# Mixture-of-experts slots on one core: the transposes of the next slot's x moved from behind gate and up to the start of the slot, and the copy of x on ScalarE moved ahead of Silu

## The chip, the cores and the metric

The kernel runs on one core of a Trainium2 chip. The metric is the device time of one execution in microseconds (us). The numbers are the median of three executions and one profiled execution, whose trace is what the rows below are read from.

## The reference

Two layers on x of 8 x 256 tokens, 512 wide: grouped-query cross attention with a residual, and then a mixture of experts with a residual. The change is in the second. Cut to what matters:

```python
h = layernorm(x).reshape(2048, 512)
logits = h @ gate_w.T                        # 32 experts
w, sel = top 4 of the softmax, normalised
for e in range(32):
    g, u = h @ Wg[e], h @ Wu[e]              # 512 -> 192
    large += (silu(g) * u * cw_large[:, e]) @ Wd[e]
for c in range(16):                          # one per pair of experts
    small += (silu(h @ cWg[c]) * (h @ cWu[c]) * cw_small[:, c]) @ cWd[c]
out = x + large + 0.05 * small
```

Only the four chosen experts of a token have a weight that is not zero.

## The kernel before, in words

The kernel has three stages in one program: attention (`attention`), routing (`route`) and the experts (`experts`, lines 1226 to 1445), where the change lies. All tiles there are float32.

Routing sorts the 2048 x 4 pairs of token and expert into slots of 128 rows that all belong to one expert, and makes tables of them: `tok` and `dst` (which row of the normalised x a place of the slot reads, and which row of the output it adds to), `slot_e` (the slot's expert) and `slot_buf` (which of the NW = 4 weight buffers of `W` holds it). In this run there are 78 slots for 32 experts. The normalised x lies in memory as `xd`, with the 32 routing weights of the row behind its 512 columns.

A slot s goes through these steps; p is s modulo 2 and picks one of two buffers:

- GpSimd, `gather` (L1285): copies the slot's column of `tok` to an index tile (L1290) and issues an indirect DMA of 128 rows into `xg[p]` (L1293). From slot 2 on it first waits for `xt_full` and `wt_ready` of slot s - 2, since `xg[p]` is used by that slot until then.
- TensorE, `transpose_x` (L1393): waits until the gather has landed (`x_loaded[p]`), then four transposes of 128 x 128 into `xt_ps[p]` (L1396).
- ScalarE, `x_evac` (L1326): copies them to `xT[p]` (L1328).
- TensorE, `gate_up` (L1399): four products for gate into `g_ps[p]` and four for up into `u_ps[p]`, each 320 columns wide, 192 of the large expert and 128 of the small one (L1403). The expert's weights are 2 MB in `W`; `experts_ready` says that they are there.
- ScalarE, `silu` (L1330): Silu of gate into `sg[p]` (L1332), released by the last product of up.
- VectorE, `gated` (L1371): `weights_of` copies the slot's routing weights out of `xg[p]` to `wt[p]` (L1369), then a = up x sg (L1374, L1375).
- TensorE, `transpose_a` (L1409): three transposes of a into `at_ps` (L1412). VectorE, `at_evac` (L1359), copies them to `aT[p]` (L1361).
- TensorE, `down` (L1415): three products of 512 columns into `y_ps` (L1420), which then counts `slots_done`.
- ScalarE, `y_evac` (L1334): scales y by `wt[p]` into `yb[p]` (L1339) and counts `y_empty`.
- GpSimd, `add` (L1296): copies the slot's column of `dst` (L1299), waits for `y_empty` and until the scatter of the slot before has landed (`y_added`), and issues an indirect DMA that adds `yb[p]` to the output (L1307).

Each engine works through its own queue in the order written, and the engines meet at semaphores only. TensorE's order within its slot s (`slot`, L1425) is the transposes of a of slot s - 1, gate and up of slot s, the transposes of x of slot s + 1, down of slot s - 1. Between them it reads `slot_e` and `slot_buf` from the tables (L1426, L1427, L1434). ScalarE's (L1341) is Silu of slot s, the copy of x of slot s + 1, the copy of y of slot s - 1. VectorE takes the transposes of a of slot s - 1, then wt and a of slot s. GpSimd issues four gathers ahead in all and then, in turn, `add` of slot k and `gather` of slot k + 4. So in TensorE's slot k + 1 down of slot k ends, its scatter and then the gather of slot k + 4 follow, and x of slot k + 4 is transposed in TensorE's slot k + 3.

SyncE (L1262) loads an expert's weights as soon as `slots_done` has reached the last slot of the expert that used the buffer before: the same end of down that releases the copy of y.

The loops run over two slots a turn, the first two slots and the last steps are written out.

Of the kernel before, what the change touches and what calls it, by code (L numbers as in the profile page):

```python
# [1225 lines left out]
def experts(nc, ident, xd, out, tabs, wts, W, w_loaded):  # L1226
# [4 lines left out]
    with ExitStack() as ctx:  # L1231
# [29 lines left out]
        @block.sync  # L1261
        def _(sp):  # L1262
            def arrived(i, p):
                sp.wait_ge(w_loaded[p], i * DMA + DMA)
                sp.sem_inc(experts_ready, 1)

            for p in range(NW - 1):
                arrived(0, p)
            with sp.Fori(1, E_ // NW) as i:
                for p in range(NW):  # L1270

                    last = sp.value_load(cum_i[0:1, bass.ds(i * NW + p - NW, 1)], min_val=1, max_val=NS)
                    sp.wait_ge(slots_done, last)
                    load_expert(sp, wts, W, w_loaded, i, p)
                    arrived(i if p else i - 1, (p - 1) % NW)
            arrived(E_ // NW - 1, NW - 1)

        def count(eng):

            return (eng.value_load(turns[0:1, 0:1], min_val=E_ // 2, max_val=NS // 2),  # L1280
                    eng.value_load(turns[0:1, 1:2], min_val=E_ - 2, max_val=NS - 2))
# [42 lines left out]
        @block.scalar  # L1324
        def _(act):
            def x_evac(s, p):  # L1326
                act.wait_ge(xt_full, s + 1)
                act.copy(xT[p][:, :, :], xt_ps[p][:, :].rearrange("p (c t) -> p c t", c=C)).then_inc(xt_empty, 1)  # L1328

            def silu(s, p):  # L1330
                act.wait_ge(gu_full, s + 1)
                act.activation(sg[p][:, :], g_ps[p][:, 0:IW], ACT.Silu).then_inc(sg_ready, 1)  # L1332

            def y_evac(s, p):  # L1334
                act.wait_ge(slots_done, s + 1)
                act.wait_ge(wt_ready, s + 1)
                if not (isinstance(s, int) and s < 2):
                    act.wait_ge(y_added, (s - 1) * DMA)  # L1338
                act.activation(yb[p][:, :], y_ps[:, :], ACT.Copy, scale=wt[p][:, :]).then_inc(y_empty, 1)  # L1339

            def slot(s, p, first=False):  # L1341
                silu(s, p)
                x_evac(s + 1, 1 - p)
                if not first:
                    y_evac(s - 1, 1 - p)

            x_evac(0, 0)
            slot(0, 0, first=True)
            slot(1, 1)
            n, last = count(act)  # L1350
            with act.Fori(1, NS // 2) as i:
                with act.If(i < n):
                    slot(i * 2, 0)
                    slot(i * 2 + 1, 1)
            y_evac(last + 1, 1)
# [35 lines left out]
        @block.tensor  # L1391
        def _(pe):
            def transpose_x(s, p):  # L1393
                pe.wait_ge(x_loaded[p], (s - p) * (DMA // 2) + DMA)
                for c in range(C):
                    m = pe.transpose(xt_ps[p][:, c * P:(c + 1) * P], xg[p][:, c * P:(c + 1) * P], ident[:, :])  # L1396
                m.then_inc(xt_full, 1)

            def gate_up(s, p, buf):  # L1399
                pe.wait_ge(xt_empty, s + 1)  # L1400
                for ps_, g in ((g_ps, 0), (u_ps, 1)):
                    for c in range(C):
                        m = pe.matmul(ps_[p][:, 0:IW], xT[p][:, c, :],  # L1403
                                      W[:, bass.ds(buf, 1), (2 * c + g) * IW:(2 * c + g + 1) * IW]
                                      .rearrange("p a f -> p (a f)"),
                                      start=(c == 0), stop=(c == C - 1))
                m.then_inc(gu_full, 1)

            def transpose_a(s, p):  # L1409
                pe.wait_ge(a_ready, s + 1)  # L1410
                for c in range(3):
                    m = pe.transpose(at_ps[:, c, :], a[p][:, c * P:(c + 1) * P], ident[:, :])  # L1412
                m.then_inc(at_full, 1)

            def down(s, p, buf):  # L1415
                pe.wait_ge(at_empty, s + 1)
                if not (isinstance(s, int) and s == 0):
                    pe.wait_ge(y_empty, s)
                for c in range(3):
                    m = pe.matmul(y_ps[:, :], aT[p][:, c, :],  # L1420
                                  W[:, bass.ds(buf, 1), GW + c * D:GW + (c + 1) * D].rearrange("p a d -> p (a d)"),
                                  start=(c == 0), stop=(c == 2))
                m.then_inc(slots_done, 1)

            def slot(s, p, first=False):  # L1425
                e = pe.value_load(slot_e[0:1, bass.ds(s, 1)], min_val=0, max_val=E_ - 1)  # L1426
                buf = pe.value_load(slot_buf[0:1, bass.ds(s, 1)], min_val=0, max_val=NW - 1)  # L1427
                if not first:
                    transpose_a(s - 1, 1 - p)
                pe.wait_ge(experts_ready, e + 1)  # L1430
                gate_up(s, p, buf)
                transpose_x(s + 1, 1 - p)
                if not first:
                    down(s - 1, 1 - p, pe.value_load(slot_buf[0:1, bass.ds(s - 1, 1)], min_val=0, max_val=NW - 1))  # L1434

            transpose_x(0, 0)
            slot(0, 0, first=True)
            slot(1, 1)
            n, last = count(pe)
            with pe.Fori(1, NS // 2) as i:  # L1440
                with pe.If(i < n):
                    slot(i * 2, 0)
                    slot(i * 2 + 1, 1)
            transpose_a(last + 1, 1)
            down(last + 1, 1, pe.value_load(slot_buf[0:1, bass.ds(last + 1, 1)], min_val=0, max_val=NW - 1))
# [58 lines left out]
```

## Time and profile before

| what | value |
|---|---|
| three executions | 1132.22 us median (1127.34 to 1135.8) |
| profiled execution | 1135.69 us |
| its span, first to last instruction | 1133.9 us |
| mean granted clock of TensorE in the span | 0.961 |
| TensorE busy (matmuls) | 1032.1 us (91%) |
| VectorE, ScalarE, GpSimd busy | 418.6, 349.3, 297.2 us |
| the expert stage | from about 510 us to the end |

How to read it: the span is cut into 40 slices of 28.3 us, and a digit is the busy share of an engine in that slice in tenths. PE is TensorE's matmuls, PEld its weight loads, DVE VectorE, ACT ScalarE, POOL GpSimd, SPq the queue of SyncE, which issues DMAs. A row of a timeline gives the start and the length of a piece in us from the span's start, the engine, the line, the operation, the tile written and those read, the number of instructions, and in brackets how long the engine was idle ahead of it and what ended that. The chain of waits goes back from a last instruction, at each step to what released it; "issue" in it is time in which an engine waited for nothing that the profile shows. A transpose on TensorE is a matmul with `ident`. In a row on stretches stand, behind the stretch and its length, the busy time of PE, PEld, DVE, ACT and POOL, the granted share of TensorE's full clock, the share of the DMA engines and GB/s. "to landing" is from the issue of a DMA to its semaphore.

### The profile page before, as it was taken

To read this page: it belongs to the slowest core of one execution; us is meant where nothing else is said; L and a number is where in the kernel's file an instruction comes from. 1 tells how busy PE (TensorE), PEld (TensorE's weight loads), DVE (VectorE), ACT (ScalarE), POOL (GpSimd) and SP (SyncE) were. 2 spreads that over 40 slices of the span, in tenths; PEclk is the share of its full clock that TensorE was granted. 3 is DMA by queue.
4 is the path that set the end of the run, shared out by engine and by line. 5 is a ranking of instruction groups with operands and counts; after the bars stand their busy time and mean duration, and the time that the engine had idled before them with its cause. 6 is when DMAs were issued, how large, how long until landed. Compare 5 with 4: busy or idle time off the path is not lost.

```text
span 1133.9 us, 19012 instructions
## 1 busy us (share of the span) xinstructions
PE 1032.1 (91%) x5518; PEld 664.7 (59%) x5520; DVE 418.6 (37%) x1039; ACT 349.3 (31%) x643; POOL 297.2 (26%) x387
## 2 busy tenths in 40 slices
PE   7689999999998979427999999999999999999995
PEld 6556666666665437215666666666665666666662
DVE  4476667766666524691111111111111111111110
ACT  2245454454545533141222222222222222222221
POOL 2101101011020000202344334334333344433432
PEclk9799999999999998757999999999999999999998
DMA  6433032130320003922765675675666667667443
GB/s 206 151 90 71 21 90 57 34 71 21 90 57 16 2 1 134 378 103 47 218 151 141 215 224 143 212 224 146 189 171 148 207 162 209 189 171 219 73 67 56
DMA packets 51449, 146.65 MB, mean 129 GB/s; under 512 B 9552, under 2 KB 18896, under 8 KB 47056
## 3 DMA queue, kind: packets, MB, share of 16 engines
q1 hardware_dynamic: 32192, 99.43, 26.3%
q0 software_dynamic: 17632, 42.74, 19.4%
q10 hardware_dynamic: 1584, 3.93, 1.0%
q8 instruction: 26, 0.43, 0.2%
q14 instruction: 15, 0.12, 0.0%
HBM read 100.73 MB, written 29.36 MB: 115 GB/s over the span
## 4 chain that ended last, share of the span: by engine, by line
PE 53%; issue 0%; DMA 0%; POOL 0%; ACT 0%; DVE 0%; POOLq 0%; ACTq 0%
PE y_ps L1420 18%; PE g_ps L1403 15%; PE u_ps L1403 15%; PE xt_ps L1396 3%; PE at_ps L1412 2%; DMA xg<-xd,gidx 0%; POOL out_x L1307 0%; ACT yb L1339 0%; ACT xT L1328 0%; DVE aT L1361 0%; ACT sg L1332 0%; DVE a L1374 0%; DVE a L1375 0%; POOL gidx L1290 0%; ACTq L1338 0%
## 5 line engine op out<-in xcount | busy, mean ns | idle before, releaser
L1420 PE MATMUL y_ps<-W,aT 128*128 x468 | 215.6, 597 | 1.1 <-DVE aT L1361 0.8
L1307 POOL DMA_INDIRECT out_x<-yb,yidx x78 | 125.3, 1606 | 297.2 <-DMA out_x<-yb,yidx 134.9
L348 ACT ACTIVATE pt<-stp 128x512 f32<-128x512 f32 x256 | 139.2, 597 | 169.4 <-PE stp L638 169.4
L470 DVE TENSOR_REDUCE mx<-s 128x2 f32<-128x512 f32 x256 | 163.0, 681 | 63.7 <-PE s L624 63.5
L1403 PE MATMUL g_ps<-W,xT 128*128 x624 | 183.3, 437 | 0.9 <-ACT xT L1328 0.9
L1403 PE MATMUL u_ps<-W,xT 128*128 x624 | 181.3, 434 | 0.0
L1403 PEld LDWEIGHTS u_ps<-W,xT 128*128 128x128 f32 x624 | 119.1, 191 | 49.9 <-issue 0.8
L1403 PEld LDWEIGHTS g_ps<-W,xT 128*128 128x128 f32 x624 | 113.5, 192 | 39.0 <-issue 2.4
L1374 DVE TENSOR_TENSOR a<-u_ps,sg 128x192 f32<-128x192 f32 x78 | 27.9, 358 | 291.5 <-ACT sg L1332 291.5
L1420 PEld LDWEIGHTS y_ps<-W,aT 128*128 128x128 f32 x468 | 83.5, 192 | 77.4 <-issue 77.3
L1332 ACT ACTIVATE sg<-g_ps 128x320 f32<-128x320 f32 x78 | 34.1, 437 | 306.2 <-PE u_ps L1403 306.2
L1361 DVE COPY aT<-at_ps 128x384 f32<-128x384 f32 x78 | 43.5, 558 | 183.3 <-PE at_ps L1412 183.3
L1339 ACT ACTIVATE yb<-y_ps,wt 128x512 f32<-128x512 f32 x78 | 53.7, 688 | 167.7 <-PE y_ps L1420 167.7
L624 PE MATMUL s<-kst,qst 96*128 96x256 bf16 x512 | 85.9, 277 | 20.4 <-DVE mx L470 19.6
L1293 POOL DMA_INDIRECT xg<-xd,gidx x80 | 80.9, 1011 | 69.8 <-POOL gidx L1290 65.8
L638 PE MATMUL stp<-qst,kst 98*128 98x256 bf16 x512 | 78.5, 276 | 8.5 <-DMA qst<-nm 8.2
L624 PEld LDWEIGHTS s<-kst,qst 96*128 96x128 bf16 x512 | 44.3, 98 | 61.8 <-DVE mx L470 41.2
L638 PEld LDWEIGHTS stp<-qst,kst 98*128 98x128 bf16 x512 | 45.2, 98 | 42.3 <-issue 33.6
L1290 POOL COPY gidx<-tok 128x1 uint32 (+1 forms) x80 | 58.4, 731 | 40.3 <-POOLq L895 29.6
L654 PE MATMUL ov<-pt,vx 128*32 128x256 f32 x1024 | 68.5, 385 | 0.0
L682 PE MATMUL side<-Wfc,oT 128*128 128x512 f32 x128 | 61.9, 599 | 1.5 <-ACT oT L338 1.5
L261 POOL TENSOR_TENSOR q<-qres,q 128x512 bf16<-128x512 f32 x14 | 16.2, 1158 | 161.7 <-DVE q L464 161.7
(172 smaller groups left out, 949.5 us busy)
## 6 DMA issues: line engine op xcount, KB each, us to landing
W<-in_wts SPq DMA_DIRECT2D x32, 2048.0 KB, 8.2
qst<-q SPq DMA_DIRECT2D x42, 256.0 KB, 4.9
ctxT<-in_ctx SPq DMA_DIRECT2D x8, 512.0 KB, 3.5
xd<-r_xn SPq DMA_DIRECT2D x16, 256.0 KB, 2.0
out_x<-xs SPq DMA_DIRECT2D x1, 4096.0 KB, 13.9
kst<-k SPq DMA_DIRECT2D x48, 64.0 KB, 2.1
xs<-in_x ACTq DMA_DIRECT2D x1, 2560.0 KB, 11.2
qst<-nm SPq DMA_DIRECT2D x128, 2.0 KB
```

Source lines behind the costliest of these rows:

```text
L348: act.activation(pt[g % 2][:, 2 * (j % 2) + r, :, :], stp[n % STP][:, :, :], ACT.Exp, scale=DH ** -0.5).then_inc(exp_done, 1)
L470: dve.tensor_reduce(mx[j // CH % 2][:, h:2 * G:G], s1[r][:, :, :], AX.X, ALU.max)\
L624: m = pe.matmul(s1[r][:, t, :], qst[b % 2][0:ROWS_QK, head(j, r), t * P:(t + 1) * P], kst[b % 2][0:ROWS_QK, head(j, r) // C, :], start=Tru ...
L638: m = pe.matmul(stp[n % STP][:, t, :], kst[b % 2][0:ROWS_ST, head(j, r) // C, t * P:(t + 1) * P], qst[b % 2][0:ROWS_ST, head(j, r), :], st ...
L654: m = pe.matmul(ov[c * VW:(c + 1) * VW, g % 2, :], vx[b % 2][:, t, g % 2 * C + c, :], pt[(b * G + g) % 2][:, c, t, :], start=(t == 0), sto ...
L682: m = pe.matmul(side[:, :], oT[t][:, c, :], Wfc[:, c, :], start=(c == 0), stop=(c == C - 1))
L1290: pool.tensor_copy(idx[p][:, :], tok[:, bass.ds(s, 1)]).then_inc(idx_ready, 1)
L1293: pool.indirect_dma_start(xg[p][:, :], None, xd[:, :], bass.IndirectOffsetOnAxis(idx[p][:, :], 0))\
L1307: pool.indirect_dma_start(out[:, :], bass.IndirectOffsetOnAxis(yidx[p][:, :], 0), yb[p][:, :], None, compute_op=ALU.add).then_inc(y_added, ...
L1339: act.activation(yb[p][:, :], y_ps[:, :], ACT.Copy, scale=wt[p][:, :]).then_inc(y_empty, 1)
L1403: m = pe.matmul(ps_[p][:, 0:IW], xT[p][:, c, :], W[:, bass.ds(buf, 1), (2 * c + g) * IW:(2 * c + g + 1) * IW] .rearrange("p a f -> p (a f) ...
L1420: m = pe.matmul(y_ps[:, :], aT[p][:, c, :], W[:, bass.ds(buf, 1), GW + c * D:GW + (c + 1) * D].rearrange("p a d -> p (a d)"), start=(c == ...
```

## The change

Two lines change places with others. On TensorE the transposes of x of slot s + 1 go from between `gate_up` and `down` to the start of the slot, ahead of the transposes of a. On ScalarE the copy of x of slot s + 1 goes ahead of Silu of slot s. Gathers, scatters, weight loads and all waits inside the steps are as they were.

```diff
@@ scalar @@
             def slot(s, p, first=False):
+                x_evac(s + 1, 1 - p)
                 silu(s, p)
-                x_evac(s + 1, 1 - p)
                 if not first:
                     y_evac(s - 1, 1 - p)
@@ tensor @@
                 buf = pe.value_load(slot_buf[0:1, bass.ds(s, 1)], min_val=0, max_val=NW - 1)
+                transpose_x(s + 1, 1 - p)
                 if not first:
                     transpose_a(s - 1, 1 - p)
                 pe.wait_ge(experts_ready, e + 1)
                 gate_up(s, p, buf)
-                transpose_x(s + 1, 1 - p)
                 if not first:
                     down(s - 1, 1 - p, pe.value_load(slot_buf[0:1, bass.ds(s - 1, 1)], min_val=0, max_val=NW - 1))
```

On TensorE, in the first of the two slots of the loop's body, this stands before the change from the last product of up on: the transposes of x (`xt_ps`), the read of the weight buffer's number, the products of down (`y_ps`), the reads for the next slot and its transposes of a (`at_ps`).

```order
L1403 MATMUL u_ps<-W,xT 128x320
L1394 ISA
L1396 MATMUL xt_ps<-ident,xg 128x128 x4
L1434 ISA
L1434 TENSOR_LOAD slot_buf
L1434 ISA x2
L1420 ISA
L1420 MATMUL y_ps<-W,aT 128x512
L1420 ISA
L1420 MATMUL y_ps<-W,aT 128x512
```

At the start of the same slot after the change, from the read of the weight buffer's number to the first product of gate (`g_ps`):

```order
L1427 TENSOR_LOAD slot_buf
L1427 ISA x2
L1394 ISA
L1396 MATMUL xt_ps<-ident,xg 128x128 x4
L1412 MATMUL at_ps<-ident,a 128x128 x3
L1431 REGISTER_ALU
L1400 REGISTER_ALU
L1403 ISA
L1403 MATMUL g_ps<-W,xT 128x320
```

The four transposes of x have moved to the front of the slot, in front of the three of a; the ones of a and all products behind them now follow the wait for the gather, which stands in front of L1396.

On ScalarE, in the same slot, before the change Silu (`sg`) is first:

```order
L1331 ISA
L1332 ACTIVATE sg<-g_ps 128x320
L1327 REGISTER_ALU
L1328 COPY xT<-xt_ps 128x512
L1338 ISA
L1339 ACTIVATE yb<-y_ps,wt 128x512
```

and after it the copy of x (`xT`) is first:

```order
L1327 ISA
L1328 COPY xT<-xt_ps 128x512
L1331 REGISTER_ALU
L1332 ACTIVATE sg<-g_ps 128x320
L1338 ISA
L1339 ACTIVATE yb<-y_ps,wt 128x512
```

The copy of y stays last.

## Rows read from the trace of the kernel before

**Rows 1.** the page: busy tenths in 40 slices; a DMA issue, us to landing
```profile
PE   7689999999998979427999999999999999999995
...
W<-in_wts SPq DMA_DIRECT2D x32, 2048.0 KB, 8.2
```

**Rows 2.** the chain of waits, 799 to 835 us: start us, us, what
```profile
801.45 0.33 PE at_ps L1412 x3
...
806.09 0.44 PE xt_ps L1396 x4
...
809.10 0.33 PE at_ps L1412 x3
```

**Rows 3.** timeline: start us, us, engine line op out<-in xcount [idle before <-releaser]
```profile
809.22 0.69 ACT L1339 ACTIVATE yb<-y_ps,wt 128x512 f32<-128x512 f32 x1 [2.07 <-PE y_ps L1420]
...
855.13 0.69 ACT L1339 ACTIVATE yb<-y_ps,wt 128x512 f32<-128x512 f32 x1 [2.07 <-PE y_ps L1420]
...
855.19 0.34 SPq L886 DMA_DIRECT2D W<-in_wts  x1
...
856.40 0.15 DVE L1369 COPY wt<-xg 128x1 f32 x1 [0.47 <-issue]
856.82 1.61 POOL L1307 DMA_INDIRECT out_x<-yb,yidx  x1 [3.31 <-ACT yb L1339]
...
859.48 1.01 POOL L1293 DMA_INDIRECT xg<-xd,gidx  x1 [0.85 <-POOL gidx L1290]
...
867.22 0.42 PEld L1396 LDWEIGHTS xt_ps<-ident,xg 128*128 128x128 f32 x4 [0.43 <-DMA xg<-xd,gidx]
...
867.40 1.60 POOL L1307 DMA_INDIRECT out_x<-yb,yidx  x1 [6.71 <-DMA out_x<-yb,yidx]
```

**Rows 4.** timeline where the expert stage begins
```profile
511.08 1.17 POOL L1293 DMA_INDIRECT xg<-xd,gidx  x1 [1.00 <-POOL gidx L1290]
...
514.85 1.12 PE L1396 MATMUL xt_ps<-ident,xg 128*128 128x128 f32 x4 [6.73 <-DMA xg<-xd,gidx]
...
516.00 0.59 ACT L1328 COPY xT<-xt_ps 128x512 f32<-128x512 f32 x1 [8.44 <-PE xt_ps L1396]
...
516.84 1.43 PE L1403 MATMUL g_ps<-W,xT 128*128 x2 [0.87 <-ACT xT L1328]
```

**Rows 5.** 520 to 1120 us: who waited for whom; landing of yb's scatters
```profile
PEld xt_ps L1396 <- DMA xg<-xd,gidx: 0.4, 1, 0.4
...
DMA to landing us min/median/max: 4.7/5.0/9.7
```

**Rows 6.** timeline of GpSimd, 815 to 875 us
```profile
841.52 1.61 POOL L1307 DMA_INDIRECT out_x<-yb,yidx  x1 [3.79 <-ACT yb L1339]
...
844.18 1.01 POOL L1293 DMA_INDIRECT xg<-xd,gidx  x1 [0.85 <-POOL gidx L1290]
...
849.66 1.60 POOL L1307 DMA_INDIRECT out_x<-yb,yidx  x1 [4.28 <-DMA out_x<-yb,yidx]
```

**Rows 7.** the chain of waits, 860 to 885 us: start us, us, what
```profile
862.66 0.33 PE at_ps L1412 x3
...
867.29 0.58 PE xt_ps L1396 x4
867.88 0.25 issue
...
871.09 0.54 PE at_ps L1412 x3
...
878.99 0.33 PE at_ps L1412 x3
```

**Rows 8.** tile W: duration ns min/median/max, first to last start
```profile
L886 SPq DMA_DIRECT2D W<-in_wts x28: 337/341/365, 541.1 to 1040.5; - x28
```

**Rows 9.** two stretches: busy us and instructions of each engine, PEclk, DMA
```profile
424.00:428.00 4.00, 0.10 (x1) 0.13 (x2) 3.03 (x22) 1.59 (x2) 2.11 (x12) 0.88 0.06 18
428.00:434.00 6.00, 6.00 (x27) 4.56 (x28) 1.94 (x5) 1.76 (x3) 0.35 (x1) 0.51 0.51 194
```

## The prediction

> **What bounds the kernel now.** I read the page's slices first. From slice 20 of 40 (about 540 us, early in the expert stage) TensorE stands at nine tenths or more in every slice but the last [rows 1]: this stage has no idle time to win back. The chain of waits over one slot [rows 2] shows why: it is TensorE alone, without a gap, three transposes of a (0.33 us), gate and up (from 801.78 to 806.09, 4.31), four transposes of x (0.44), down (from 806.53 to 809.10, 2.57), 7.65 us from one at_ps to the next. There are 78 slots. So the change can only win if something else becomes shorter, and its danger is a wait put in front of TensorE, which works in its written order.
>
> Which wait ends last once x is wanted at the slot's start? I followed one x row set back on the timeline [rows 3]. A slot boundary (the end of down) lies 0.12 us ahead of yb's copy, from 809.10 in [rows 2] against the copy at 809.22; here 855.13 - 0.12 = 855.01. Call it T. GpSimd has one queue: scatter of slot k, then the index copy and the gather for slot k + 4. The scatter waits for yb(k), which down(k) releases at T, the end of slot k + 1. It issues at 856.82 (T + 1.8), the gather at 859.48 (T + 4.5). Its x is transposed in slot k + 3. Before, that is behind gate and up of slot k + 3, at T + 7.65 + 0.33 + 4.31 = T + 12.3; after, at the start of that slot, T + 7.65. The slack for a landing falls from 12.3 - 4.5 = 7.8 us to 3.2 us.
>
> What a landing takes: the first gather, with no other kernel work on the engines, is issued at 511.08 and TensorE starts on it at 514.85, 3.8 us later [rows 4]. The gather of [rows 3], issued 4.3 us behind a 2 MB weight load (855.19), needs 867.22 - 859.48 = 7.7 us. Even the shortest is beyond 3.2. Before, the second just fits: in the whole stage TensorE waited for a gather once, 0.4 us [rows 5].
>
> **The change part by part.** It removes and adds no matmul or copy. The slot's 7.65 us of work are the same; so is the work on ScalarE.
>
> Copy of x ahead of Silu: price 0. The transposes that release it now end 4.3 us ahead of up, so Silu is still released by up, and the copy takes its place in ScalarE's idle time. Queued behind it are Silu and the copy of y; the y copy waits for down at the slot's end anyway. It can't win either: the transposes of a are covered as before, by down and the x transposes.
>
> Transposes of x ahead of those of a: behind the new wait stand the transposes of a, gate and up and down, all of the slot. The gathers themselves do not come earlier. Their buffer is free earlier, but what holds them is the scatter in front of them on GpSimd's queue, which hangs on the end of down.
>
> Slot without a weight load: landing at T + 4.5 + 3.8 = T + 8.3, wanted at T + 7.65, late by 0.6.
>
> Slot with a load: the load is released by the same end of down (855.19 beside the yb copy), lasts 8.2 us [rows 1], and so lies over scatter and gather. A usual one, also behind a load, is [rows 6]: the scatter of 841.52 holds the next one until 849.66. In [rows 3] the scatter of 856.82 holds its follower until 867.40, and the gather had landed at 867.22, 0.2 earlier. So a usual loaded gather lands about 849.66 - 0.2 = 849.5, which is 5.3 us after its issue at 844.18 (an estimate from those rows). T + 4.5 + 5.3 = T + 9.8, late by 2.1. Ends: 3.8 (no effect of the load) and 7.7. Scatters, from issue to landing, have a median of 5.0 and a maximum of 9.7 [rows 5], the latter being the one of [rows 3]; I take 5.3 for the usual ones. Six GpSimd waits for a scatter's landing are 5.6 us or longer (one of them stands in [rows 3], 6.71) where a usual one is 4.3 [rows 6]; for these six I add 1.7 us, late by 3.8.
>
> Restart: a TensorE queue that has run empty needs time to run ahead again. In [rows 7] the x transposes start on time (867.29) but their landing was just in time, and the two slots take 878.99 - 862.66 = 16.33 us instead of 15.30, 1.0 us lost: x transposes 0.58 instead of 0.44, 0.25 before down, where the weight buffer's number is read from a table, a transposes 0.54 instead of 0.33. In the new order 4.3 us of gate and up lie between the wait and that table read, so of these I take only 0.14 and 0.21 and a rest of 0.05: 0.4 per late landing; bounds 0 and 1.0.
>
> How lateness adds up: a gather hangs on the end of slot k + 1 and is wanted at the start of slot k + 3, so a wait at the start of slot k + 2 shifts the demand and not the gather. The wait of a slot is its lateness less the wait of the slot before. So a loaded slot pays fully (2.1 + 0.4 = 2.5), and the unloaded one behind it pays almost nothing. Almost, since GpSimd's index copy waits also for wt, which VectorE makes after the transposes of a (856.40 + 0.15, T + 1.5, after the change 0.44 plus the wait later); I put 0.15 on each slot behind a load. Unloaded slots in a row pay half of 1.0. There are 28 loads between 541 and 1041 us [rows 8], one in 2.3 slots: mostly every second, some every third. A third slot's wait is taken off the next loaded slot, so its sum is nothing.
>
> Start: transposes of x(1) now stand ahead of the first gate and up, at half clock, 1.1 us where the copy of x(0) leaves 0.8 free between 516.0 and 516.84 [rows 4]; the second gather was issued at about 513.3. I put 0.8; 0 to 2 bound it.
>
> Sum: 22 usual loads x 2.5 = 55; 6 long ones x (3.8 + 0.4) = 25; 28 slots behind loads x 0.15 = 4; about 12 unloaded slots at the ends x 0.5 = 6; start 1; what the kernel before loses in [rows 7] and two smaller places, -1 to -2. Together 90. The profiled execution took 1135.7 us, so 1225.7; it is 3.5 above the median of 1132.2, so about 1222 for a median.
>
> **The rivals.** First, the waits are smaller. With a restart of 0 and loaded landings of 4.5 us, between the two measured ones but near the short end, a loaded slot pays 4.5 + 4.5 - 7.65 = 1.3: 28 x 1.3 = 37 and nothing elsewhere, 1169. For it: GpSimd's times in a profile are rough. Against: 8.3 us for the unloaded landing come from two plain rows.
>
> Second, not slower: the landing of a lone gather is shorter than it looks in [rows 4], since the time from issue to start there holds TensorE's own waking too. The place is the start of every slot, the price 0 as long as a landing takes less than 7.65 - 4.5 - 0.4 = 2.8 us; then only the start is left, less the 1.0 us of [rows 7], 1132. Against: 3.8 and 7.7.
>
> Third, TensorE's clock falls. In [rows 9] TensorE does almost nothing for 4 us (424 to 428) and the next 6 us run at 0.51, the level of 1.2 GHz. Such a stretch costs 3 us. My six long waits are near 4 us: 6 x 3 = 18, 1240. If every load's wait did it, 28 x 3 = 84, 1306. Against: usual waits of 2.1 us stand between more than 7 us of work. The Trainium skill, TensorE: Matmul & The Clock Gate, section on HAM oscillation, holds that a wait for a DMA on every tile can throttle the array again so that each tile starts cold. By that rule the 28 or all slots would run partly at the low level; the trace before has no such repeated wait to test it.
>
> **How the numbers follow.** Forecast 0.72; smaller waits 0.11; clock 0.10; not slower 0.07. Within the forecast, restart 0 and the six long ones priced as usual ones take off 0.4 x 28 + 10 = 21 and lead to 1201; a restart of 1.0 adds 17, and half of the usual loads at the long price 19 more, 1258. To reach the rivals in part, the range is 1180 to 1260. A measurement here tells about 1% from no change. Faster by over 1% 0.02, within 1% 0.05, slower 0.93.
>
> **What would show it.** In the trace after: weight loads of TensorE for xt_ps end waits on the gather in most slots (some 50 of 78, about 60 to 80 us in all, against 0.4); slots with a load last about 10.2 us, those behind them 7.7 to 7.9; GpSimd's waits for the scatter's landing become rarer, since slots grow; gather issues stay 4.5 us behind the end of down; TensorE's digits fall from 9 to 8 in the loop. Wrong it would be if the xt_ps waits were few, if they occurred but the slots without loads stayed at 7.65 throughout, or if the granted clock left 1.0 between 530 and 1110 us.

## The result, and the profile after

The changed kernel takes 1214.78 us in the median of four executions (1213.48 to 1221.76), against 1131.64 before: a ratio of 1.0748, 95% interval 1.0703 to 1.0792, so 7.5% slower. The profiled execution took 1216.07 us, 80.4 more than the one before. The text on record says 1222, with a range of 1180 to 1260.

The page of the changed kernel, the two rows that answer to [rows 1] and the span:

```profile
span 1214.3 us, 19012 instructions
...
PE   7699999999999792398988889898989988998995
...
PEclk9899999999999986599999999999999999999998
```

From slice 20 on digits of 8 stand among the nines, where before there were nines only. Matmuls whose ends are modelled hide a part of the gaps, so the list of who waited for whom says more (us in total, times, longest; 520 to 1200 us, to be read beside [rows 5]):

```profile
PEld xt_ps L1396 <- DMA xg<-xd,gidx: 105.7, 54, 3.2
POOL out_x L1307 <- DMA out_x<-yb,yidx: 100.3, 23, 4.6
...
PE xt_ps L1396 <- DMA xg<-xd,gidx: 65.8, 44, 2.4
...
POOL gidx L1290 <- DVE wt L1369: 25.7, 28, 9.2
```

TensorE's matmuls stood idle for 65.8 us ahead of transposes of x, in 44 waits, and its weight loads for 105.7 us; before the change the latter were 0.4. The longest wait of a matmul was 2.4 us. The two lists count the same waits on two queues and are not to be added: what moves the time is the one of the matmuls. The scatters, for which GpSimd waited 134.9 us before, now cost it 100.3: slots are longer, and more of them have landed when the next is due. The index copy waits for wt in 28 cases; apart from a first one of 9.2 us before the loop, some 0.6 each.

How one slot looks, on the timeline from 803 to 822 us (start, length, what, and the idle time in front with its end):

```profile
803.84 0.60 PE L1396 MATMUL xt_ps<-ident,xg 128*128 128x128 f32 x4
...
808.46 1.01 POOL L1293 DMA_INDIRECT xg<-xd,gidx  x1 [0.84 <-POOL gidx L1290]
...
811.77 0.69 ACT L1339 ACTIVATE yb<-y_ps,wt 128x512 f32<-128x512 f32 x1 [2.22 <-PE y_ps L1420]
811.83 18.18 SPq L886 DMA_DIRECT2D W<-in_wts  x2
...
812.11 0.66 PE L1396 MATMUL xt_ps<-ident,xg 128*128 128x128 f32 x4 [0.46 <-DMA xg<-xd,gidx]
...
813.46 1.61 POOL L1307 DMA_INDIRECT out_x<-yb,yidx  x1 [3.79 <-ACT yb L1339]
...
816.12 1.01 POOL L1293 DMA_INDIRECT xg<-xd,gidx  x1 [0.85 <-POOL gidx L1290]
...
820.10 0.69 ACT L1339 ACTIVATE yb<-y_ps,wt 128x512 f32<-128x512 f32 x1 [2.22 <-PE y_ps L1420]
...
821.60 0.66 PE L1396 MATMUL xt_ps<-ident,xg 128*128 128x128 f32 x4 [1.62 <-DMA xg<-xd,gidx]
```

An unloaded slot first. The gather issued at 808.46 is wanted at the boundary, 811.77 - 0.12 = 811.65, and TensorE starts on it at 812.11, 3.65 us after the issue and 0.46 idle. Then a loaded one: the weight load starts at 811.83, the scatter at 813.46 (T + 1.8), the gather at 816.12 (T + 4.5, T = 811.65), and TensorE starts at 821.60, 5.5 us after the issue. The boundary is at 820.10 - 0.12 = 819.98; 1.62 us are lost. These two are usual ones: over the whole stage, of the gathers that TensorE waited for, the 28 behind a load account for 55.6 us of waits and the 16 others for 10.1. From issue to TensorE's start, 26 of the 28 take 5.3 to 5.6 us, and the 16 others have a median of 3.8 (3.6 to 4.9). What follows costs little more (chain of waits of the changed kernel, start us, us):

```profile
821.60 0.66 PE xt_ps L1396 x4
822.26 0.33 PE at_ps L1412 x3
...
829.47 0.44 PE xt_ps L1396 x4
```

The transposes of x take 0.66 instead of 0.44, those of a 0.33 as ever, and the slot goes from 819.98 to 829.47, 9.49 us: 7.65 + 1.62 + 0.22.

In five slots there is one thing more. Two stretches around one of the longer waits (columns as in [rows 9]), and the two rows of the timeline at that place:

```profile
677.00:681.00 4.00, 1.76 (x11) 0.93 (x10) 0.00 (x0) 0.85 (x2) 0.73 (x1) 1.00 0.58 155
681.00:685.00 4.00, 4.00 (x11) 2.66 (x10) 0.71 (x2) 0.42 (x1) 2.27 (x4) 0.57 0.51 66
```

```profile
680.14 0.66 PE L1396 MATMUL xt_ps<-ident,xg 128*128 128x128 f32 x4 [2.24 <-DMA xg<-xd,gidx]
...
680.96 3.90 PE L1403 MATMUL g_ps<-W,xT 128*128 x8
```

The transposes had to wait 2.24 us, and some 1.4 us after they have begun the granted clock falls to the 1.2 GHz level for 3.4 us (0.57 in the mean over 681 to 685; the moment and the length are from the trace's record of the clock). At the other four it falls between 0.1 us ahead of the transposes' start and 1.4 us behind it. Gate takes 3.90 us there; in a slot at full clock, here one of the timeline from 793 us on, it is 2.32:

```profile
796.95 2.32 PE L1403 MATMUL g_ps<-W,xT 128*128 x8
```

With 0.1 to 0.2 us more in up, each of the five costs about 1.7 us, together 8.5 of the 80.4 us. All five stand at waits of 2.1 to 2.4 us; 13 other waits of over 2 us and all the shorter ones left the clock alone. Four of the five lie between 530 and 1110 us, where the clock was at its full value before the change and is now 0.99 in the mean:

```profile
530.00:1110.00 580.00, 520.15 (x1916) 324.44 (x1915) 83.82 (x266) 109.87 (x198) 198.35 (x264) 0.99 0.58 159
```

### The profile page after: what moved, and what is told of

Read it like the earlier page. It is cut to its first block, busy times and chain, and to the rows that moved or that the text cites. A ratio compares the mean times of both kernels' runs of the same rounds, so it can differ in the third digit from the quotient of the medians.

```text
span 1214.3 us, 19012 instructions
## 1 busy us (share of the span) xinstructions
PE 1045.1 (86%) x5518; PEld 667.7 (55%) x5520; DVE 418.4 (34%) x1039; ACT 345.6 (28%) x643; POOL 296.1 (24%) x387
## 4 chain that ended last, share of the span: by engine, by line
PE 28%; DMA 16%; issue 7%; POOL 3%; ACT 2%; DVEq 1%; POOLq 1%; DVE 0%; ACTq 0%
DMA xg<-xd,gidx 16%; PE y_ps L1420 8%; PE g_ps L1403 8%; PE u_ps L1403 7%; PE xt_ps L1396 3%; POOL gidx L1290 2%; PE at_ps L1412 2%; ACT yb L1339 1%; POOL out_x L1307 1%; DVEq L1365 1%; DVE wt L1369 0%; POOLq L1299 0%; POOLq L1290 0%; DVE aT L1361 0%; POOLq L1291 0%
## 5 line engine op out<-in xcount | busy, mean ns | idle before, releaser
L1403 PE MATMUL g_ps<-W,xT 128*128 x624 | 190.0, 449 | 0.0
L1403 PEld LDWEIGHTS g_ps<-W,xT 128*128 128x128 f32 x624 | 117.3, 198 | 40.2 <-issue 5.3
L1420 PEld LDWEIGHTS y_ps<-W,aT 128*128 128x128 f32 x468 | 89.5, 191 | 89.5 <-issue 77.3
L1396 PE MATMUL xt_ps<-ident,xg 128*128 128x128 f32 x316 | 51.7, 288 | 73.3 <-DMA xg<-xd,gidx 73.3
L1396 PEld LDWEIGHTS xt_ps<-ident,xg 128*128 128x128 f32 x316 | 36.6, 144 | 127.7 <-DMA xg<-xd,gidx 113.9
L1293 POOL DMA_INDIRECT xg<-xd,gidx x80 | 80.7, 1008 | 69.8 <-POOL gidx L1290 65.8
L1328 ACT COPY xT<-xt_ps 128x512 f32<-128x512 f32 x79 | 46.0, 582 | 72.2 <-PE xt_ps L1396 71.3
```

The lines of the kernel that those rows point to most:

```text
L1293: pool.indirect_dma_start(xg[p][:, :], None, xd[:, :], bass.IndirectOffsetOnAxis(idx[p][:, :], 0))\
L1403: m = pe.matmul(ps_[p][:, 0:IW], xT[p][:, c, :], W[:, bass.ds(buf, 1), (2 * c + g) * IW:(2 * c + g + 1) * IW] .rearrange("p a f -> p (a f) ...
L1420: m = pe.matmul(y_ps[:, :], aT[p][:, c, :], W[:, bass.ds(buf, 1), GW + c * D:GW + (c + 1) * D].rearrange("p a d -> p (a d)"), start=(c == ...
```

## The experiments

The theory on record, G: TensorE has been put behind a gather that hangs on the end of down through GpSimd's queue. The rivals: A, ScalarE's order costs; T, TensorE's new order costs by itself; and for a single run that the loads have no part or that the number of buffers is what counts.

**Half the change, ScalarE.**

```diff
             def slot(s, p, first=False):
+                x_evac(s + 1, 1 - p)
                 silu(s, p)
-                x_evac(s + 1, 1 - p)
```

> Only ScalarE's half of the change: the copy of x ahead of Silu, TensorE as before. Theory G (the late gather: TensorE is put behind a gather that hangs on the end of down through GpSimd's queue) expects no change, 1131 us within 4: after up come 0.44 us of transposes, the copy 0.59, Silu 0.44 and a 0.64, 2.1 in all, and the transposes of a are due 0.44 + 2.58 = 3.0 us after up. Rival A (ScalarE's new order costs) expects a part of the 83 us here, over 10 us.

Measured: 1134.8 us, ratio 1.0036 (1.0018 to 1.0055). Rival A is out as a cause of the loss: 2 to 6 us at most stand here. That the interval lies just above 1 stays unexplained; the profiled execution of this kernel spans 1132.9 us, 1.0 less than the one before.

**Half the change, TensorE.** The other lines of the diff alone.

> Only TensorE's half of the change: the transposes of x first, ScalarE as before. Theory G expects the whole loss, 1215 us within 5. Rival A expects it to be clearly below 1205.

Measured: 1225.2 us (1216.4 to 1227.2), ratio 1.081 (1.0759 to 1.086). The whole loss is here, and 10 us more than with both halves, beyond what I expected. The waits for x are nearly the same, 67.4 us against 65.8:

```profile
PE xt_ps L1396 <- DMA xg<-xd,gidx: 67.4, 44, 2.7
```

What differs is the clock. From the groups by line, 520 to 1200 us (busy us, mean ns of one), first of the changed kernel, then of this one:

```profile
L1403 PE MATMUL g_ps<-W,xT 128*128 x619 | 187.3, 447 | 0.0
```

```profile
L1403 PE MATMUL g_ps<-W,xT 128*128 x611 | 192.6, 462 | 0.0
```

Gate's products take 447 ns in the mean and here 462 (434 before the change). Counted in the trace's granted clock over the slots, it fell 10 times here and 5 times in the changed kernel, 3.4 us each, which at 1.7 us apiece is 8 of the 10 us. The waits have much the same length in both (20 and 18 of them are over 2 us); why one takes the clock down and the next does not was not tested, and that ScalarE's order has a part in it is not shown. The four executions here took 1216.4 to 1227.2 us, with a mean granted clock of 0.958 in the shortest and 0.950 to 0.952 in the others.

**x wanted 0.33 us later.**

```diff
-                transpose_x(s + 1, 1 - p)
                 if not first:
                     transpose_a(s - 1, 1 - p)
+                transpose_x(s + 1, 1 - p)
```

> As the changed kernel, but the transposes of x directly behind those of a, so x is wanted 0.33 us later in each slot. Theory G: each of the 28 waits behind a weight load is 0.33 us shorter and the others by about half that, 10 to 13 us less than the changed kernel, 1203. Rival T (not the gather's time but TensorE's new order costs, by its refilled queue or its clock) expects 1215, since the order of the waits is the same kind.

Measured: 1209.7 us, ratio 1.0702 (1.0672 to 1.0733), 5 less than the changed kernel by the medians, where I expected 10 to 13. The waits fell as they should, by 9.8 us:

```profile
PE xt_ps L1396 <- DMA xg<-xd,gidx: 56.0, 42, 2.4
```

The direction is that of theory G and not T; the medians fell by less than the waits, in executions that scatter by several us. The two profiled executions, with five falls of the clock each, differ by 8.7 us (1207.4 against 1216.1).

**x wanted between gate and up.**

```diff
                 for ps_, g in ((g_ps, 0), (u_ps, 1)):
+                    if g:
+                        transpose_x(s + 1, 1 - p)
                     for c in range(C):
```

> The transposes of x between gate and up, x wanted at T + 7.65 + 0.33 + 2.15 = T + 10.1 us (T: the end of down that releases scatter and gather). Theory G: loaded gathers land at T + 9.9, so 28 x 0.2 = 5 us, and up to 9 more if six long landings come back, 1136 to 1146. Rival T expects well above 1150, since TensorE still takes x ahead of most of the slot's products.

Measured: 1138.9 us, ratio 1.0083 (1.0051 to 1.0116), as theory G had it. The clock did not fall before the last slots, and five waits are left in the profiled execution:

```profile
PE xt_ps L1396 <- DMA xg<-xd,gidx: 4.1, 5, 1.4
```

Three positions of the same four transposes, at the start of the slot, 0.33 us and 2.5 us behind it, give 1215, 1210 and 1139, and at 4.6 us 1131. That is a due time against a landing.

**Without the weight loads.** In the expert loop of SyncE:

```diff
                     sp.wait_ge(slots_done, last)
-                    load_expert(sp, wts, W, w_loaded, i, p)
-                    arrived(i if p else i - 1, (p - 1) % NW)
-            arrived(E_ // NW - 1, NW - 1)
+                    sp.sem_inc(experts_ready, 1)
+            sp.sem_inc(experts_ready, 1)
```

> The kernel before without the 28 weight loads of the expert stage: the experts from the fifth on use the first four experts' weights, so this part of the computation is wrong. Theory G and its rivals: 1129 to 1131 us, since TensorE sets the time and waited for gathers in three places only (about 2 us).

> The changed kernel without the 28 weight loads (experts from the fifth on use the first four's weights). Theory G: every slot is then an unloaded one, late by 0.4 to 0.6 us plus 0.2 to 0.4 of restart, half of it per slot, 76 x 0.3 to 0.5 = 23 to 38 us over the kernel before without loads, 1155 to 1168. So more than half of the loss goes with the loads. A rival (loads have no part, the chain through GpSimd's queue costs the same in each slot) expects 1205 or more; rival T expects the loss to stay too.

Measured: 1129.2 us for the order of before (ratio 0.9979, 0.9952 to 1.0006) and 1167.2 for the changed one (1.0317, 1.0289 to 1.0346). So of 83 us, 38 are there without any load and 45 to 48 come with them; of these the clock is 8.5, since without loads it did not fall between 530 and 1140 us. The matmuls' waits without loads are:

```profile
PE xt_ps L1395 <- DMA xg<-xd,gidx: 24.7, 45, 1.4
```

That is 45 waits in 77 slots, 0.5 us each in the mean and none over 1.4. In the others there is none: the lateness is paid in one slot and then shifts the next demand, as the working says.

**The gather ahead of the scatter.** GpSimd alone (beside these lines `tok` gets two more columns of zeros, VectorE counts `wt_ready` once more at its end, and the last wait is for one gather more):

```diff
-            for s in range(4):
+            for s in range(5):
                 gather(s, s % 2)
             add(0, 0)
...
-                        gather(i * 2 + p + 2, p)
+                        gather(i * 2 + p + 3, 1 - p)
                         add(i * 2 + p - 1, 1 - p)
```

> The changed kernel with GpSimd's gather of slot k + 4 ahead of the scatter of slot k instead of behind it. The gather then hangs on wt of slot k + 2 (about 2.0 us into that slot), is issued 1.6 us later and lands at 2.0 + 1.6 + 3.6 = 7.2 us when no load runs, just in time, and 0.9 to 1.5 us late with one. Theory G: 28 x 0.8 to 1.5 = 22 to 42 us, 1153 to 1173. If the scatter in front of the gather is not what delays it, 1210 or more.

Measured: 1239.7 us, ratio 1.0951 (1.0913 to 1.0989). This is slower than the changed kernel, on the side of "1210 or more" and far from 1153 to 1173. The timeline at a loaded slot:

```profile
795.33 0.34 SPq L886 DMA_DIRECT2D W<-in_wts  x1
...
797.30 0.18 POOL L1290 COPY gidx<-tok 128x1 uint32 x1 [2.67 <-DVE wt L1369]
...
798.33 1.01 POOL L1293 DMA_INDIRECT xg<-xd,gidx  x1 [0.85 <-POOL gidx L1290]
...
806.44 0.66 PE L1397 MATMUL xt_ps<-ident,xg 128*128 128x128 f32 x4 [3.64 <-DMA xg<-xd,gidx]
```

The order does what it should: the gather is issued 3.0 us behind the load instead of 4.3. But it needs 806.44 - 798.33 = 8.1 us instead of 5.5, lands 11.1 us behind the load's issue instead of 9.8, and TensorE waits 3.64 us here. That is the commoner case and not the only one: of the 28 gathers issued 2.9 to 3.1 us behind a load, 18 take 6.6 to 8.8 us and 10 take 5.2 to 5.8. What parts the two groups is open. The loads land later as well, 10.5 us behind their issue in the median where it is 8.1 in the changed kernel.

Two rows say where the time went: the waits of the matmuls (520 to 1190 us), and the mean granted clock over the slots (the third number from the end):

```profile
PE xt_ps L1397 <- DMA xg<-xd,gidx: 70.5, 28, 4.3
```

```profile
530.00:1190.00 660.00, 589.47 (x2105) 372.46 (x2104) 92.08 (x291) 119.64 (x218) 215.68 (x288) 0.95 0.56 148
```

The waits are only 5 us more than in the changed kernel (65.8). The larger part of the difference is the clock: it fell at 15 of the 28 waits and stood at its lower level for 65 us, which costs 32 us against 8.5. The same kernel without loads shows what its order is worth when the loads are away:

> The kernel with the gather ahead of the scatter (two buffers), without the 28 weight loads (experts from the fifth on use the first four's weights). In the run with loads, 26 gathers took 5 to 8.7 us and it came out 1240 us instead of the 1153 to 1173 expected. If the loads alone are behind that: gathers of 3.3 to 4 us, issued 3.1 us into a slot, land before the next slot begins, 1131 to 1140. If the order itself costs: over 1150.

Measured: 1133.5 us, ratio 1.0023 (1.0004 to 1.0042). Against the two runs without loads (0.9979 and 1.0317) the moved gather takes away all but about 5 us of the 38, and matmuls wait for no gather at all; weight loads of TensorE do, a little:

```profile
PEld xt_ps L1396 <- DMA xg<-xd,gidx: 9.3, 34, 0.5
```

So the scatter in front of the gather is what makes an unloaded gather late. The load is a second cause, and the clock, which falls at the longer waits, adds to its price.

**Four buffers.** `xg`, its index tiles and its semaphores four instead of two, the loops of TensorE, VectorE and GpSimd written out over four slots, and a gather waits for slot s - 4 to be free; once with the gather ahead of the scatter, once behind it, and once with TensorE's and ScalarE's order of before:

```diff
-        xg = [sb(f"xg{i}", [P, XW], F32) for i in range(2)]
+        xg = [sb(f"xg{i}", [P, XW], F32) for i in range(4)]
...
-                if not (isinstance(s, int) and s < 2):
-                    pool.wait_ge(xt_full, s - 1)
-                    pool.wait_ge(wt_ready, s - 1)
+                if not (isinstance(s, int) and s < 4):
+                    pool.wait_ge(xt_full, s - 3)
+                    pool.wait_ge(wt_ready, s - 3)
...
-                        gather(i * 2 + p + 2, p)
-                        add(i * 2 + p - 1, 1 - p)
+                            gather(m * 4 + (k + 3), (k + 3) % 4)
+                            add(m * 4 + (k - 1), 1 - p)
```

> The changed kernel with four buffers for the gathered x instead of two and the gather of slot k + 4 ahead of the scatter of slot k, so that a gather is issued almost a slot and a half ahead of its use on either engine order. The loop is written out over four slots. Theory G: the wait is gone and with it the loss, 1129 to 1134 us. Rival T (the new order itself, its refills and clock falls): stays above 1160.

> The changed kernel with four buffers for the gathered x, but the gather of slot k + 4 behind the scatter of slot k as before. Theory G says that the gather hangs on the scatter in front of it, not on a free buffer: no change against the changed kernel, 1215 us within 6. Rival: the buffers are what four_buffers gained by, then about 1130.

> TensorE's and ScalarE's order of before, with four buffers and the gather ahead of the scatter as in four_buffers. Theory G: both orders are then free of waits for x, so 1128 to 1131 us like four_buffers (1129.1), and the transposes' place is worth nothing by itself, within 3 us.

Measured: 1129.1 us with the changed order and the gather ahead (ratio 0.9981, 0.9951 to 1.001); 1221.7 with the gather behind the scatter (1.0763, 1.0727 to 1.08); 1129.85 with the order of before and the gather ahead (0.9984, 0.997 to 0.9999). With four buffers but the old place in GpSimd's queue (`k + 2` where the diff has `k + 3`) the waits are those of the changed kernel to 0.4 us:

```profile
PE xt_ps L1401 <- DMA xg<-xd,gidx: 66.2, 43, 3.0
```

The time lies 0.7 us outside the 1215 within 6 that I had expected; the clock fell 11 times in the profiled execution. So buffers alone do nothing, the place in the queue alone does nothing good under loads, and both together take the whole loss away with TensorE's and ScalarE's new order left as it is. Rival T falls with this run. Between the two orders there is then no difference that can be measured: the transposes' place has no worth of its own. Both kernels with four buffers and the gather ahead are 0.2% below the kernel before, which is at the edge of what these runs resolve and fits the 1 to 2 us that the kernel before loses, 1.0 of them in [rows 7].

**The load later.** In the changed kernel:

```diff
+                    sp.wait_ge(gu_full, last + 2)
                     sp.wait_ge(slots_done, last)
                     load_expert(sp, wts, W, w_loaded, i, p)
```

> The changed kernel with each weight load issued later: not at the end of the expert's last down (T) but when up of the slot behind it is done, about T + 5.1, 0.6 us behind the issue of the gather at T + 4.5 instead of 4.3 us ahead of it. The load lies then over T + 5.1 to T + 13.3, and the next slot's gather is issued at about T + 12.6. Theory G with a landing that depends on what of a load lies in front of the gather: both gathers land after 3.6 to 4.5 us, so most of the 48 us that the loads cost (1214.8 against 1167.2 without them) goes, 1167 to 1190. Rival: the load takes the same time from the gathers wherever it lies, 1210 or more.

Measured: 1260.2 us in the median of four (1238.8, 1254.3, 1266.1 and 1270.2); the ratio of 1.1029 (1.0944 to 1.1115) is of the two shorter ones, and the profiled execution is the longest. The expectation was wrong. The rival has the time right, 1210 or more, but not the reason, since the load takes more from the gathers here and not the same. From the timeline:

```profile
796.06 1.01 POOL L1294 DMA_INDIRECT xg<-xd,gidx  x1 [0.84 <-POOL gidx L1291]
...
796.85 0.33 SPq L886 DMA_DIRECT2D W<-in_wts  x1
...
803.85 1.11 PE L1397 MATMUL xt_ps<-ident,xg 128*128 128x128 f32 x4 [4.61 <-DMA xg<-xd,gidx]
```

The gather is issued 0.8 us ahead of the load and all the same TensorE starts 7.8 us after the issue, after 4.61 us idle. The transposes then take 1.11 us, the clock being down. In the whole trace, 15 gathers issued 0.8 us ahead of a load take 6.6 to 8.8 us, six issued 1.0 to 1.5 us ahead take 4.6 to 5.1, and eight issued 6.9 us behind one take 3.8 to 4.8. The clock fell at all 16 waits of 3.4 to 6.6 us, 85 us at the lower level in all, which is 43 us of the loss of this execution.

The packets of the DMA queues show why an early issue does not help. q1 carries SyncE's loads (without them it has 58.7 MB less), q0 GpSimd's gathers and scatters. The rows are queue, packets, MB and share of the 16 DMA engines. First the changed kernel from 812 to 818 us, then from 818 to 821:

```profile
q1 hardware_dynamic: 114, 1.87, 85.1%
```

```profile
q0 software_dynamic: 221, 0.54, 70.9%
q1 hardware_dynamic: 30, 0.23, 18.9%
```

The load of 811.83 moves alone up to 818. Nothing of GpSimd's moves in this time, though its scatter was issued at 813.46 and its gather at 816.12; both follow when the load is nearly through. In gather_first it is the same from 797.5 to 802 us, all 93 packets are the load's, and the gather issued at 798.33 starts behind them. So for a gather issued behind a load the end of the load counts more than the time of its own issue. In load_late both move at once, here from 798 to 803 us:

```profile
q1 hardware_dynamic: 95, 1.56, 74.3%
q0 software_dynamic: 74, 0.25, 23.0%
```

The gather of 796.06 comes behind the scatter in front of it: the first of its 64 packets starts at 797.8, the load's first at 798.2, so that 53 of the 64 run between those of the load, up to 802.7. Its issue was ahead of the load, its data was not. Why the queues share the DMA engines in the one case and not in the other stays open.

## Why the prediction was right

The mechanism and the place were right, each by a run of its own: the wait is for the gather (four_buffers), it hangs on GpSimd's queue behind the scatter (gather_first_no_loads, four_behind), the load adds to it (after_no_loads), ScalarE's half is nearly free (act_only). The total came out 10 us too high in the profiled executions, 90 against 80.4, and 7 in the medians, 1222 against 1214.8. That the number is so near is in part luck: what the terms on record stand for came to 73 us, 17 less than their 90, and 8.5 us of clock, which are in none of them, fill half of that gap. Term by term:

- Landing of an unloaded gather: T + 8.3 on record; 4.46 + 3.65 = T + 8.1 in the row above, and T + 8.3 with the median of 3.8.
- A loaded gather: 5.3 us on record, 5.5 measured. The wait of the row above is 1.62 since the slot before had waited 0.46; together 2.1, as on record. "The wait of a slot is its lateness less the wait of the slot before" holds to 0.1.
- The six long landings: priced at 25 us, and there were none. The longest wait of a matmul is 2.4 us, the longest on record for them was 3.8. This is the largest single miss, 6 x 1.7 = 10 us. In the trace before, the load behind each of the six had come only two slots (15.3 us) after the load before it, but so had those of many usual ones; in the changed kernel two slots with a load among them last 17.8 us (the merged row of 18.18 us in the timeline above ends with the issue of the next load, which takes 0.34). I had no reason in the rows to think that they would vanish, and that the spacing is the cause was not tested.
- Restart: 0.4 on record, 0.22 measured. The part of the x transposes was 0.22 (taken as 0.14), that of the transposes of a nothing (taken as 0.21). Over 44 late slots that is 10 us; on record it is 11 in the 28 loaded slots and 2 to 3 in the others, about 14.
- The clock: a rival with 0.10 on record, for waits near 4 us, 18 us in all. It came for five of the 18 waits of over 2 us, at 1.7 each, 8.5 us, beside the forecast and not in its place. I had taken the stretch of [rows 9] for the kind of wait that it needs; it was only the one that the old trace held. By the Trainium skill (TensorE: Matmul & The Clock Gate, on HAM oscillation) a wait for a DMA at every tile, of some 3 to 5 us in its case, takes the clock down again and again; the trace of the changed kernel agrees in part, 5 of 44 waits of up to 2.4 us. In gather_first, with waits of up to 4.3 us, it was 15 of 28, and in load_late all 16 of 3.4 us and more, the one of 4.61 us above among them.
- Start: 0.8 on record; from the first gather's issue to the first copy of y it is 531.95 - 510.04 = 21.9 us where it was 533.28 - 511.08 = 22.2, so nothing.
- Slots behind a loaded one: 28 x 0.15 = 4 us on record. By the intervals between copies of y they last 7.65 us, 0.1 over in all 28 together, so the wait for wt on GpSimd cost nothing there. The other slots without a load: 6 us on record; the 21 of them are 14 us over 7.65 each in sum, 10.1 of it waits.

Waits of 65.8, restarts of 44 x 0.22 = 9.7, the clock's 8.5, less the 2.3 that the kernel before loses itself and the 0.3 of the start, are 81.4. The stages ahead of the experts were 1.0 us shorter in this execution (the first gather at 510.04 and not 511.08), which leaves the 80.4.

The signs put on record: waits of weight loads for x in 54 slots (some 50 were expected, 60 to 80 us; they are 105.7 on PEld and 65.8 on PE, where the text should have said on which). Waits of GpSimd for the scatter are rarer, 23 where there were 31, and gathers stand still 4.5 us behind the end of down. Slots with a load last 10.1 us in the median, as expected (10.2), those behind them 7.65 and not 7.7 to 7.9. One of the signs of being wrong came true: the granted clock left 1.0 between 530 and 1110 us, four times. By its own sign the forecast therefore does not hold whole; the third rival is in it with 8.5 of the 80.4 us, and the late gather has the rest.

## What to carry to other kernels

An engine that is busy all the time, as TensorE here, gained nothing from a new order of its work and lost by it. So ask for each moved step what its operand hangs on, follow that back through the other engine's queue to the event that releases it, and compare due time and landing. Here 7.8 us of slack became 3.2 by a move of two lines, and the old trace showed no more of it than one wait of 0.4 us. If such a step is to go forward, its load has to be freed from what stands in front of it in its queue, and has to have a buffer to go to; with the loads running either alone did not help. And a second transfer beside it can decide when it lands, more than its own issue does: look at the packets by queue.

## What the runs showed of the hardware

- A gather of 128 rows takes 3.6 to 4.9 us from its issue to TensorE's start with no load near (median 3.8), 5.3 to 5.6 us if issued 4.3 us behind a 2 MB load (26 gathers), 5.2 to 5.8 or 6.6 to 8.8 us if issued 3.0 us behind it (10 and 18 of 28), and 6.6 to 8.8 us if issued 0.8 us ahead of it. These are the gathers that TensorE waited for.
- While the load of 811.83 us ran, from 812 to 818, no packet of GpSimd's queue moved, with a scatter and a gather issued in that time.
- TensorE's granted clock fell to its lower level for 3.4 us at five of 44 waits of up to 2.4 us, each time 1.7 us more; in the run with TensorE's half alone, with nearly the same waits, ten times. The four executions of that run differ by up to 0.9%. With waits of up to 4.3 us it fell at 15 of 28, and from 3.4 to 6.6 us at all 16.
